# Fused token mixer, attention and MLP on one core: new order of the setup, half of the diagonal Gram products, own banks for a half-chunk

## What is computed

```python
# x: (2, 1, 4096, 256), two batches; d_gamma: (4096, 4096)
q = x @ Wq + bq;  k = x @ Wk + bk;  v = x @ Wv + bv
scores = einsum('btd,bsd->bts', q, k)
y = einsum('bts,bsd->btd', d_gamma * scores, v) @ Wo + bo
h = where(y >= 0, y, prelu_a * y)                       # tokenizer
mn = layernorm(layernorm(h)) * gamma + beta             # attention, between the two batches
att = softmax(einsum('slhc,tlhc->sth', mn @ Wq2, mn @ Wk2) * scale)
h = h + (einsum('sth,tlhc->slhc', att, mn @ Wv2) * sigmoid(mn @ Wg2 + bg)) @ Wo2 + bo2
# MLP: half of each batch's tokens, chosen by a router, pass gelu(n @ w1 + b1) @ w2 + b2
```

## Time and profile before

| | |
|---|---|
| median of 3 runs | 2058.73 us (2057.74 to 2061.1) |
| the profiled execution | 2060.18 us, of which the span of its instructions is 2058.5 |
| PE busy | 1986.8 us, 97% of the span |
| DVE, ACT, POOL busy | 1219.7, 675.1, 453.7 us |
| mean granted clock of TensorE | 0.981 |

### The profile page before, as it was taken

How to read it: one execution, slowest core, us unless ns; L and a number is a source line. 1 busy time by engine, 2 the same in 40 slices (tenths; PEclk the granted TensorE clock), 3 DMA queues, 4 the chain that set the end, 5 groups by cost and what they waited for, 6 DMA issues and landing times.

```text
span 2058.5 us, 27479 instructions
## 1 busy us (share of the span) xinstructions
PE 1986.8 (97%) x9534; PEld 1644.2 (80%) x9534; DVE 1219.7 (59%) x2220; ACT 675.1 (33%) x1094; POOL 453.7 (22%) x578
## 2 busy tenths in 40 slices
PE   7999999999999999999999999999999989939998
PEld 6888888888888888888888878888887878828897
DVE  4646565655656566766565656556565348866553
ACT  4422222222222225422222222222222237625554
POOL 3302020202102022321020202112021247623442
PEclk8999999999999999999999999999999989969999
DMA  4232433333243333232433333342434449712110
GB/s 144 82 110 69 162 122 123 113 122 121 93 163 108 128 113 133 82 120 96 164 103 133 113 123 102 122 153 83 143 112 142 170 174 312 272 60 59 42 42 32
DMA packets 88114, 250.14 MB, mean 122 GB/s; under 512 B 11968, under 2 KB 32448, under 8 KB 88000
## 3 DMA queue, kind: packets, MB, share of 16 engines
q1 hardware_dynamic: 84928, 240.27, 34.9%
q0 software_dynamic: 3072, 8.44, 1.3%
HBM read 194.05 MB, written 54.62 MB: 121 GB/s over the span
## 4 chain that ended last, share of the span: by engine, by line
PE 90%; DVE 4%; issue 2%; ACT 2%; POOL 1%; DMA 0%; SPq 0%; DVEq 0%; ACTq 0%; POOLq 0%
PE bank L663 35%; PE bank L678 34%; PE bank L1581 4%; PE bank L810 4%; PE bank L1602 4%; PE bank L713 3%; PE bank L1174 2%; PE bank L635 1%; PE bank L609 1%; PE bank L619 1%; DVE kt L482 0%; DVE vf L493 0%; PE bank L648 0%; ACT work L380 0%; PE bank L836 0%
## 5 line engine op out<-in xcount | busy, mean ns | idle before, releaser
L678 PE MATMUL bank<-x_hi,kt 128*128 128x512 f32 x2048 | 724.2, 396 | 1.5 <-DVE work L519 1.4
L519 DVE SCALAR_TENSOR_TENSOR work<-bank,d_col,gate 128x512 f32<-128x512 f32 x512 | 384.0, 750 | 554.0 <-PE bank L678 544.9
L398 ACT ACTIVATE p_hi<-work 128x512 fp32r<-128x512 f32 x512 | 324.1, 633 | 1066.0 <-PE bank L663 1023.0
L678 PEld LDWEIGHTS bank<-x_hi,kt 128*128 128x128 f32 x2048 | 384.3, 188 | 90.8 <-DVE work L519 2.6
L663 PE MATMUL bank<-p_hi,v_hi 128*128 128x512 f32 x1024 | 407.1, 398 | 0.3 <-ACT yT L360 0.2
L663 PE MATMUL bank<-p_hi,v_lo 128*128 128x512 f32 x1024 | 404.0, 394 | 0.0
L663 PE MATMUL bank<-p_lo,v_hi 128*128 128x512 f32 x1024 | 403.4, 394 | 0.0
L678 PE MATMUL bank<-x_lo,kt 128*128 128x512 f32 x1024 | 401.1, 392 | 0.0
L507 DVE TENSOR_TENSOR p_lo<-work,p_hi 128x512 fp32r<-128x512 f32 x512 | 367.6, 718 | 29.2 <-ACT p_hi L398 29.1
L568 POOL TENSOR_SCALAR spread<-mv 128x4 f32<-128x4 f32 x16 | 4.9, 308 | 1125.8 <-DVE mv L451 1125.8
L663 PEld LDWEIGHTS bank<-p_hi,v_hi 128*128 128x128 f32 x1024 | 192.2, 188 | 50.7 <-DVE p_lo L507 5.3
(11 more groups left out here) (227 smaller groups left out, 2275.2 us busy)
## 6 DMA issues: line engine op xcount, KB each, us to landing
gate<-in_gateT SPq DMA_DIRECT2D x256, 512.0 KB, 3.6
work<-in_xT SPq DMA_DIRECT2D x32, 512.0 KB, 4.6
scratch_rows<-rows SPq DMA_DIRECT2D x16, 518.0 KB, 3.7
scratch_h<-work SPq DMA_DIRECT2D x16, 512.0 KB, 3.0
scratch_mn<-mn_sb SPq DMA_DIRECT2D x16, 512.0 KB, 6.7
scratch_mT_hi<-mT_hi SPq DMA_DIRECT2D x16, 512.0 KB, 2.7
scratch_mT_lo<-mT_lo SPq DMA_DIRECT2D x16, 512.0 KB, 4.0
gate<-scratch_mn SPq DMA_DIRECT2D x16, 512.0 KB, 4.3
```

Source lines behind the costliest of these rows:

```text
L398: nc.scalar.activation(p_hi[:, i % 2, :], p32[:, i % RP, :], ACT.Copy).then_inc(hi_done, 1)
L519: nc.vector.scalar_tensor_tensor(p32[:, i % RP, :], S[i % 2][:, :], d_col[:, i:i + 1], gate[:, g % RG, j, :], ALU.add, ALU.mult).then_inc( ...
L678: mm = pe.matmul(S[i % 2][:, :], w, x, start=n == 1, stop=n == 3 * KD)
```

## The change

Three places are rewritten; what is computed stays the same.

1. **Setup.** The query weights get two more columns that hold bq (`wq_b`), so that A's product also gives Wk bq. The bias columns are loaded by ACT's queue (five loads) instead of SP's; the six loads that setup doesn't need (gamma, beta, attn_bo, prelu, bo, wr) are issued by SP in the first projection, behind the gate loads. x is loaded ahead of Wv and Wo. POOL, not DVE, makes the bias rows. The last four products, the bias of V (`value_bias`), are issued behind the first key projection.
2. **Gram.** n0^T n0 and n1^T n1 are symmetric: instead of high by high, high by low and low by high, PE sums half of high by high and high by low, a matrix T whose sum with its transpose is the product. ACT writes four tiles of 1024 columns per chunk in place of one of 2048: the high parts (`g_own` of n0, `g_other` of n1) and half of them (`g_other` of n0, `g_own` of n1). The head adds T and its transpose by two more products for the logits (six in place of four).
3. **Mix.** The second half-chunk's values and gates go to the banks 1, 0, 2 and 3 (`V_first`, `GB_first`) and are issued by the head behind the logits. The first half-chunk of chunk 1 then waits for 2 blends instead of 4. POOL's tables are filled once the Gram stage is over, ahead of the softmax.

```diff
 # setup_weights
+            for t, name in ((wq_b[:, :, 0:D], "tok_WqT"), (wkT[:, :, :], "tok_WkT")):
+                sp.dma_start(t, ins[name].rearrange("(k p) n -> p k n", p=P)).then_inc(qk_loaded, 16)
             sp.dma_start(x32, ins["xT"][0, 0]).then_inc(x_ld, 16)
...
-            dve.wait_ge(loaded, 16 * n_loads)
-            dve.wait_ge(made, 3)
...
         def _(act):
+                for t, name, sem in ((wq_b[:, :, D], "tok_bq", bq_ld), (wq_b[:, :, D + 1], "tok_bq", bq_ld),
+                                     (bk2[:, :, 0], "tok_bk", bk_ld), (bk2[:, :, 1], "tok_bk", bk_ld),
+                                     (bv1[:, :, 0], "tok_bv", bv_ld)):
+                    act.dma_start(t, ins[name].rearrange("(k p) -> p k", p=P)).then_inc(sem, 16)
...
             pe.wait_ge(qk_loaded, 32)
+            pe.wait_ge(bq_ld, 32)
...
+        def value_bias(pe):
             pe.wait_ge(rows, 2 * KD)
...
 # tokenizer, PE's project
                     if early(c, 1):
+                        if b == 0:
+                            value_bias(pe)
                         pe.wait_ge(w_lo, 2)
...
 # tokenizer, ACT's gram
-                nc.scalar.activation(g_hi[:, h], g32[:, h], ACT.Copy).then_inc(g_hi_ok, 1)
+                for tile, s, half in ((g_own, 0, 1.0), (g_other, 1, 1.0), (g_other, 0, 0.5), (g_own, 1, 0.5)):
+                    nc.scalar.activation(tile[:, h, s], g32[:, h, s], ACT.Copy, scale=half).then_inc(g_hi_ok, 1)
...
 # tokenizer, PE's gram
                 pe.wait_ge(g_lo_ok, c + 1)
+                pe.wait_ge(g_hi_ok, c * 4 + 4)
...
+                        pe.matmul(G[m][:, 0:2 * D], high, g_other[:, h, :, tile], start=first, stop=False, skip_group_check=True)
+                        pe.matmul(G[m][:, 0:2 * D], high, g_lo[:, h, :, tile], start=False, stop=False, skip_group_check=True)
+                        pe.matmul(G[m][:, D:2 * D], low, g_other[:, h, 1, tile], start=False, stop=False, skip_group_check=True)
...
+                        pe.matmul(G[2 + m][:, 0:D], high, g_own[:, h, 1, tile], start=first, stop=False, skip_group_check=True)
+                        mm = pe.matmul(G[2 + m][:, 0:D], high, g_lo[:, h, 1, tile], start=False, stop=False, skip_group_check=True)
...
+def mix_banks(M, c, j):
+    return (M["V_first"], M["GB_first"]) if (c, j) == (0, 1) else (M["V"], M["GB"])
...
 # head_weights
-        for i, (g0, c0, w) in enumerate(((0, 0, wk), (0, D, wq), (0, D, wk), (2, 0, wk))):
+        for i, (g0, c0, w) in enumerate(((0, 0, wk), (0, 0, wq), (0, D, wq), (0, D, wk), (2, 0, wk), (2, 0, wq))):
...
         pe.matmul(attp, heads_in["same_head"][:, :], cols[:, :], start=True, stop=True).then_inc(att_ok, 1)
+        values_and_gates(pr, pe, W2, M, 0, 0, 1)
...
 # mix, SP and PE
-            sp.wait_ge(pr.sem("hw_tp"), 4)
+            sp.wait_ge(pr.sem("hw_tp"), 6)
...
+                    if c == 1:
+                        pe.wait_ge(o_ok, 2)
+                        values_and_gates(pr, pe, W2, M, c, h, 0, (1, 2))
...
 # mix, POOL
-            pool.wait_ge(pr.sem("hw_step"), 8)
...
+            pool.wait_ge(pr.sem("g_done"), NC)
...
+            pool.wait_ge(pr.sem("hw_step"), 8)
+            nc.gpsimd.memset(power[:, :], -0.5).then_inc(power_ok, 1)
```

More of the change, by code:

```diff
@@ L82, in setup_weights @@
         a_f, vo_f = sb(nc, ctx, "a_f", [P, KD, D]), sb(nc, ctx, "vo_f", [P, KD, D + 2])
[L83 to L87, removed]
+        pa, pv, (pb, pr_) = pr.banks[0:2], pr.banks[2:4], pr.banks[6:8]
+        (qk_loaded, vo_loaded, bq_ld, bk_ld, bv_ld, made, rows, prod, kept, hi_ok, lo_ok) = (
+            pr.sem("w_" + n) for n in ("qk_loaded", "vo_loaded", "bq_ld", "bk_ld", "bv_ld", "consts", "rows", "products",
+                                       "kept", "hi", "lo"))
         x_ld, x_hi_ok, x_lo_ok = pr.sem("xp_ld0"), pr.sem("xp_hi"), pr.sem("xp_lo")
@@ L93, in _ @@
         def _(sp):
-            for t, name, sem in ((wqT, "tok_WqT", qk_loaded), (wkT, "tok_WkT", qk_loaded),
-                                 (wvT, "tok_WvT", vo_loaded), (wo, "tok_Wo", vo_loaded)):
-                sp.dma_start(t[:, :, :], ins[name].rearrange("(k p) n -> p k n", p=P)).then_inc(sem, 16)
+            for t, name in ((wq_b[:, :, 0:D], "tok_WqT"), (wkT[:, :, :], "tok_WkT")):
+                sp.dma_start(t, ins[name].rearrange("(k p) n -> p k n", p=P)).then_inc(qk_loaded, 16)
             sp.dma_start(x32, ins["xT"][0, 0]).then_inc(x_ld, 16)
[L98 to L107, removed]
+            for t, name in ((wvT, "tok_WvT"), (wo, "tok_Wo")):
+                sp.dma_start(t[:, :, :], ins[name].rearrange("(k p) n -> p k n", p=P)).then_inc(vo_loaded, 16)
         @block.gpsimd
@@ L115, in _ @@
                                     base=0, pattern=[[-1, P]], channel_multiplier=1).then_inc(made, 1)
+            pool.wait_ge(bq_ld, 32)
+            pool.wait_ge(bv_ld, 16)
+            for k in range(KD):
+                nc.gpsimd.tensor_scalar(bq_rows[:, k, :], ones[:, :], wq_b[:, k, D:D + 1], None, ALU.mult).then_inc(rows, 1)
+                nc.gpsimd.tensor_scalar(bv_rows[:, k, :], ones[:, :], bv1[:, k, 0:1], None, ALU.mult).then_inc(rows, 1)
         @block.vector
@@ L182, in _ @@
             last.then_inc(prod, 1)
+        return value_bias
 def gram_view(work, D):
@@ L310, in project @@
                             load_gate(0, b * NC, g)
+                    if early(c, 1) and b == 0:
+                        for n, name in (("gamma", "attn_gamma"), ("beta", "attn_beta"), ("attn_bo", "attn_bo"),
+                                        ("prelu", "tok_prelu_a")):
+                            sp.dma_start(W[n][:, :], ins[name].partition_broadcast(P)).then_inc(pr.sem("w_rows_ld"), 16)
+                        with nc.allow_non_contiguous_dma(reason="a bias column, once"):
+                            sp.dma_start(W["bo_col"][:, :], ins["tok_bo"].rearrange("(k p) -> p k", p=P)).then_inc(
+                                pr.sem("w_rows_ld"), 16)
+                        sp.dma_start(W["wr"][:, :], ins["ffn_wr"].partition_broadcast(P)).then_inc(pr.sem("wr_ld"), 16)
                 chunks(sp, b, project)
@@ L542, in gram @@
             def gram(c, h):
-                dve.wait_ge(g_hi_ok, c + 1)
-                nc.vector.tensor_tensor(g_lo[:, h], g32[:, h], g_hi[:, h].bitcast(F32), ALU.subtract).then_inc(g_lo_ok, 1)
+                for s, tile in enumerate((g_own, g_other)):
+                    dve.wait_ge(g_hi_ok, c * 4 + s + 1)
+                    low = nc.vector.tensor_tensor(g_lo[:, h, s], g32[:, h, s], tile[:, h, s].bitcast(F32), ALU.subtract)
+                low.then_inc(g_lo_ok, 1)
                 if early(c, 1):
@@ L839, in _ @@
         pe.wait_ge(made, 2 + P // head)
-        for i in range(4):
+        for i, of in enumerate((0, 0, 1, 2, 3, 3)):
             pe.wait_ge(prod_ok, i + 1)
```

124 lines of the change are left out of this document (63 added, 61 removed).

## The result

The changed kernel takes 2036.38 us (median of 4 runs, 2033.49 to 2038.61) beside 2058.99 of the kernel before in the same session (2057.74 to 2061.1): ratio 0.989, interval 0.9878 to 0.9902, 22.6 us less. 2033.7 was forecast, with a range of 2029 to 2042. The profiled execution of after took 2033.49 us, the fastest of the four, 26.7 less than that of before. That is more than the medians differ by: the setup, which the experiments show to vary by up to 2.8 us between executions of the same code, was at its fastest here. PE is busy for 1969.4 us, 97% of the span as before, at a mean granted clock of 0.984.

The account below looks back on a forecast made before the run. PE was taken to set the pace in the score loops, left unchanged; gains lay at setup and from Gram to first projection. 8.3 + 13.7 - 6.05 + 9.0 = 25.0 us off, median 2058.73 to 2033.7, range 2029 to 2042.

Parts of the forecast that it names:

- Setup: 8.3 forecast: Setup: the first value product starts at 19.0 instead of 27.3 us, 8.3 gained (4.6 to 12.0).
- I take the middle, 5.2: Setup: PE's first product starts at 5.2 us, when the second bq column lands, at worst 5.9.
- the rival of the bias columns: Setup: second bq column lands 4 us later, at 9.2; setup gains 4.3, kernel takes 2037.7 us; 10 in 100.
- Gram: 13.7 forecast: Gram stage: seven chunks give 1.86 us each and the first 0.7, 13.7 gained (10.0 to 14.9).
- weight loads don't set the pace: Rival: weight loads set the Gram stage's pace, gaining 7.8 instead of 13.7 us, kernel 2039.6; 6 in 100.
- ACT's four tiles: Rival: ACT's tiles follow PE's last Gram chunk, a chunk takes 11.1 us, kernel 2066.3; 3 in 100.
- the weights for the values and gates: Rival: these weights come late behind the Gram stage, 3.7 us lost, kernel 2037.4; 6 in 100.
- Head: 6.05 forecast: Head: six products instead of four cost 3.45 us, 48 narrow passes instead of 32 cost 2.6; 6.05 lost (5.5 to 9.4).
- My 10 us for all at half clock: Head: if all 48 narrow passes ran at half clock they would take 10 us and cost 5.9 more.
- Mix: 9.0 forecast: First mix chunk: the projection starts 14.0 us behind the column sums instead of 23.0, 9.0 gained (6.5 to 9.4).
- now they would land 7.6 after the sums: Mix: chunk 1's tokens land 7.6 us after the column sums, leaving PE 5.8 us for its products, just in time.
- My own mark for a wrong forecast: Mix: the forecast is wrong if chunk 1's tokens land more than 8 us after the column sums.

Follow-up runs that it names:

- the first experiment: The kernel before with the setup part of the change alone: 2051.27 us, ratio 0.9966 to before.
- the experiment with DVE's additions: The changed kernel with chunk 1's tokens ahead of the MLP's weights, and DVE adding each symmetric sum's two products (32 narrow passes, not 48): 2032.93 us, ratio 0.9877.
- the one with 21.0: The changed kernel with A's products without the columns of bq, and Wk bq as four narrow products behind them: 2036.07 us, ratio 0.9886.
- the last experiment: The changed kernel with DVE's second split first, tokens ahead of the MLP's weights, DVE's additions and nine extra products ahead of A: 2027.3 us, ratio 0.9855.
- the second experiment: The kernel before with the Gram part alone (half diagonal products and the six head products): 2050.55 us, ratio 0.9966 to before.

## Why the prediction was right, step by step

**Sum.** 25.0 us were forecast and 22.6 measured between medians (26.7 between the two profiled executions). The mechanisms were right in all three places. The terms were off by 0.8 to 2.9 us and partly cancel: in the two profiled executions the setup gave 2.9 more than forecast and the head took 0.8 less, while Gram stage and mix gave 1.7 and 1.0 less. That the sum came this near is in part luck.

**Setup: 8.3 forecast, 8.4 to 11.2 in the profiles, 7.9 alone between medians.** The wait for the slope went, and nothing took its place: the splits and the bias rows are hidden as I had it. "I take the middle, 5.2" for the first product was too early: it starts at 6.2. That is 0.3 beyond the worst bound, 5.9, and a fourth of what the rival of the bias columns supposed. The column was issued at 1.34 and took 4.75 us, so the bound was nearly right and the middle was not; and the weights alone would have held PE until 5.89. The Trainium skill's rule in "DMA: Bandwidth & Descriptors", section "Issuing engines are not separate DMA queues", speaks for such a delay. The trace agrees that the weights came later: WkT's median from issue to landing was 3.1 us before and 4.6 after. Whether it comes from the columns or from x, which now stands third in SP's queue, no run here separates. What made up for the late start is the pace: I had A at the 3.78 of before and the narrow passes, Vo, the key products and the bias of V between slow and fast. A took 3.37 in after (3.78 in most runs); but Vo took 1.97 for the 2.60 forecast, the key products 2.9 for 3.9 and the bias of V 1.2 for 2.0. In the seven profiles with after's setup, the first experiment's among them, Vo took either 1.97 us or 3.5 to 3.6: there were two paces, and the middle values that I took were neither.

**Gram: 13.7 forecast, 12.0 and 13.5 measured.** The term has the right parts: 6.53 us a chunk, and PE idle for 2.00 us after the first, named as DVE's order. What it lacks is the price of that idle time on the clock: in after the second chunk ran at 0.55, about 1.6 us more. By its length the stage did so in six of the eight executions that have this wait (57.9 to 58.0 us) and not in two (56.4). In before the waits at this place were 1.74 and 0.49 us with the clock at 1.00 behind them, and I put nothing for the clock behind a wait of 2. The rivals didn't come about: products of 512 columns keep 0.23 us apart, so weight loads don't set the pace; ACT's four tiles take 3.9 us and run beside PE's last chunk; the weights for the values and gates are there in time.

**Head: 6.05 forecast, 5.3 measured.** 10.37 us for the six groups, as forecast; the 48 narrow passes took 6.24, where I had 6.8. Their price was misread: I took the 4.19 us of 32 passes in before as full clock. The column sums of before and after (columns as in the experiment with DVE's additions):

```profile
L845 PE MATMUL bank<-hw_ones,hw_prod x32: 167/251/354, 1658.8 to 1662.8; 128*128 128x2 f32 x32
L869 PE MATMUL bank<-hw_ones,hw_prod x48: 168/251/353, 1639.7 to 1645.5; 128*128 128x2 f32 x48
```

Both hold passes of 0.35 us, and the granted clock is 0.81 and 0.85 over the sums. Where the longest pass takes 0.25, 32 take 3.5 us and 48 take 5.3. So 6.24 is what 48 take when the clock falls on the way, and the surcharge for that stood already in the 4.19. My 10 us for all at half clock don't follow from the 1.02 that I named for four (which gives 12.2), but from the 0.86 between the starts of two such groups in before. Most of the low mean clock of 0.83 lies behind the sums: the products there still start slowly, 1.05 us for two of the second half-chunk until 1650.6 and 0.63 later.

**Mix: 9.0 forecast, 8.0 measured.** POOL's first gating came 6.0 us after the sums, as forecast (5.9). The step that failed is "now they would land 7.6 after the sums": it was 9.0, of which 0.7 is the shorter column sums and 0.7 the longer way of the tokens (15.1 us from SP's release at 1639.85, not 14.4). "Just in time" left no margin, and the tokens became the wait, 0.57 us here (none to 0.6 in other executions of this mix), 2.0 in the mix alone and behind the faster Gram stage. My own mark for a wrong forecast, more than 8 us, was passed, and the loss, about 1 us, stayed inside the 2.5 I had allowed.

**Open:** when PE changes its pace in the setup. In after passes of 256 and 258 columns start 0.43 us apart at first and 0.22 later, and so it is in the profiles of all kernels with the new setup: the change comes once and stays. It comes at 9 to 10.5 us in seven profiles, at 14 to 15 in the two whose first value product starts at 18.6 and 18.9, at 17.6 in the one with 21.0, and ahead of A in the last experiment, with 15.4, where all passes of A are fast. So this moment, and not the code, makes most of the spread of the setup's gain. 0.43 us is also the pace of such passes in before at a granted clock of 0.50 (the bias of V, 2.05 us for four). It looks as if PE ran at 1.2 GHz up to that moment, but the clock column reads 1.00 there, so this is argued, not shown; and no run shows what sets the moment.

## What to carry to other kernels

When a long stage gets shorter, look for the first piece of its follower that is issued by an unrelated release: here a load that stood behind other loads held PE for 0.6 us in the changed kernel and for 2.0 where the stage ahead was shorter, and cost one moved line to free. A split on an engine with idle time belongs in front of that engine's longer work if a busier engine waits for it. And where one profiled execution is 3 us better than its median, compare the starts of the stages in several profiles before a gain is put down to a part.

## What the runs showed of the hardware

The same idle time of 2.0 us on PE was followed by a granted clock of 0.55 to 0.57 for some 4 us in after and in two further profiles, and by 1.00 in the second experiment, whose stage is the same to 0.01 us up to that point. In the setup the same eight passes of A took 3.37, 3.52 and 3.78 us without earlier work on PE, and 3.78 and 1.98 us in two executions with it, all with a granted clock of 1.00 in the record: there the pace of the products tells more than the clock column. In the head the granted clock fell although PE had no gap: over the 48 passes of 2 columns it was busy all the time, and the clock was 0.85 in the mean there and 0.50 behind them, until about 1650 us.
